# First attention in an audio tower: one sequence on 32 rows, four sequences side by side

## The chip, the cores and the metric

The kernel runs on one NeuronCore of a Trainium2 chip. The metric is the device time of one execution in microseconds (us), the median of several runs. A core has TensorE (matrix products, in the profile PE, its weight loads PEld), VectorE (DVE), ScalarE (ACT), GpSimd (POOL) and SyncE (SP), which run on their own and wait for one another by semaphores.

## The reference

64 sequences of 23 tokens go through a token layer, an attention with decaying gates, a routed feed-forward layer, a second attention and a quantized feed-forward layer. The change is in the first attention, which has 8 key heads of 128 dimensions, each with two query heads:

```python
logG = jnp.cumsum(log_g, axis=1)                       # per sequence and head
qk = jnp.einsum('bthd,bshd->bhts', q, k) * scale
a = qk ** 2
gate = logG[:, :, :, None] - logG[:, :, None, :]
a = jnp.where(causal, a * jnp.exp(gate), 0.0)
norm = jnp.sum(a, axis=-1) + 1e-06
y = jnp.einsum('bhts,bshd->bthd', a, v)
y = y / jnp.transpose(norm, (0, 2, 1))[..., None]
return y.reshape(B, T, H * R * D) @ Wc + bc            # q, k, v are hidden_states @ Wq, Wk, Wv
```

## The kernel before

The 1472 tokens (T) are four chunks (CH) of 368 columns (CW), and a chunk is 16 sequences of 23 (SL). The loop runs over the 8 heads, and its body is written out for the four chunks, on each engine in its own order. g counts chunks over all heads.

Products with weights are exact to about fp32: each operand is a high and a low fp16 part, and `split3` makes three matmuls (lines 915 to 917). `head_project(g, c, j)` projects one of q0, q1, k, v (j = 0 to 3) of a chunk: 12 matmuls of 368 columns, into bank j % 2. `out_proj(g, c)` multiplies a finished chunk's result with Wc: four blocks of 6 matmuls, into banks 6 and 7 by turns. VectorE adds each block to the accumulator (`accumulate`, line 1553). `out_proj` waits at line 973 before each block until VectorE has added the block two before it, which used the same bank.

Four sequences (92 rows, AT) are handled as one block: scores for the 92x92 pairs, of which a mask leaves the causal ones within a sequence. In a chunk TensorE does the projections that are left (j from 2 or 1), scores (line 1000, k stationary, fp32), turns v (line 1006), the previous chunk's `out_proj`, the weighted sums of v (line 1021; the stationary operand is the weight matrix, and v has a 129th column of ones, so that the sum of weights comes with it), one projection of the next chunk, and then turns the results (line 1037). ScalarE moves q, k, v out of PSUM (`head_moved`, line 661), makes E = exp(gate) (674) and the square (677), moves the turned v (680) and the turned results as yT_hi (698). VectorE makes the gates (1570, 1574), the weights a = sq x E (1579), divides the results by their sums (1593 to 1595) and makes yT_lo (1601).

Other work stands in the same order: ScalarE and VectorE split weights for the next head (`unit_a_hi`, `unit_a_lo` to wa; `unit_b_hi`, `unit_b_lo` to wb) and of an expert in every second chunk (line 666, and `expert_lo` in three pieces, line 1387), and ScalarE sums absolute values (686). In the fourth chunk TensorE waits for wa_lo before it projects for the next head. The gates reach VectorE through memory: SP writes lgt to lgd and reads it back as gr, spread over the rows (lines 406, 408 and 419). A semaphore target counts from a start value: b_acc and b_ev start at 2, b_wc at 1; free(n) is n + 1 and ready(n) is n + 3.

## Time and profile before

| | us |
|---|---|
| median of three runs | 1438.3 |
| these runs | 1438.11 to 1441.32 |
| the profiled execution | 1435.07 |
| its span (first to last instruction) | 1433.3 |
| TensorE busy in the span | 1279.8 |
| VectorE busy | 915.9 |
| ScalarE busy | 639.1 |
| GpSimd busy | 231.4 |

The profile is of one execution. Its timeline gives each instruction's start, its duration, and in brackets how long the engine had been idle and who released it. Matmuls overlap, so a stream of them is read by the distance of starts, not by durations. A product of fp32 operands shows two records.

### The profile page before, as it was taken

What the parts mean: (1) busy time and instruction counts of PE and PEld (TensorE: products, weight loads), DVE (VectorE), ACT (ScalarE), POOL (GpSimd) and SP (SyncE); (2) the same over time, 40 slices, a digit from 0 to 9 for tenths busy, and PEclk for the clock granted to TensorE, in tenths of its full rate; (3) what the DMA queues carried; (4) which work ended last, traced back from release to release, by engine and by line L of the source; (5) the groups of instructions that cost most, each with busy time, mean ns of one, the idle gap of its engine ahead of it and who ended that gap; (6) DMA issues with size and microseconds to landing.
All of it is one profiled execution on the core that took longest, in us unless ns stands there. A gap on an engine that the chain in (4) does not pass through costs nothing.

```text
span 1433.3 us, 28634 instructions
## 1 busy us (share of the span) xinstructions
PE 1279.8 (89%) x9689; PEld 789.5 (55%) x9690; DVE 915.9 (64%) x1920; ACT 639.1 (45%) x1086; POOL 231.4 (16%) x280
## 2 busy tenths in 40 slices
PE   6999999999999999996789999999986787859997
PEld 2447667677676767664435444544533565424443
DVE  5993665656656665668864555445348676778886
ACT  3444444554444445542325444444532433246664
POOL 2220000000000000000013333333347610110000
PEclk9997999999999999995799999999997787889999
DMA  5211452433435352422325867876336620000000
GB/s 191 73 66 62 161 199 104 182 135 143 182 141 199 123 191 103 176 89 83 141 75 200 280 220 246 318 256 208 109 121 137 100 36 2 1 0 16 22 22 26
DMA packets 42699, 184.21 MB, mean 129 GB/s; under 512 B 8688, under 2 KB 9200, under 8 KB 34832
## 3 DMA queue, kind: packets, MB, share of 16 engines
q0 software_dynamic: 19744, 95.41, 20.1%
q1 hardware_dynamic: 19440, 75.41, 14.8%
q10 hardware_dynamic: 3456, 12.58, 2.5%
q8 instruction: 39, 0.64, 0.2%
q14 instruction: 20, 0.16, 0.0%
HBM read 135.65 MB, written 47.73 MB: 128 GB/s over the span
## 4 chain that ended last, share of the span: by engine, by line
PE 58%; DVE 19%; issue 11%; DMA 4%; POOL 3%; ACT 2%; DVEq 1%; SPq 0%; ACTq 0%; POOLq 0%
PE ps L915 14%; PE ps L917 14%; PE ps L916 14%; PE ps L1021 3%; PE ps L1000 3%; DMA wide<-wsp 2%; DVE ff L2022 2%; DVE amf L2029 1%; PE ps L1105 1%; PE ps L1037 1%; POOL h L519 1%; PE ps L1358 1%; DVE bst L1460 1%; PE ps L1340 1%; DVE wa_lo L1387 1%
## 5 line engine op out<-in xcount | busy, mean ns | idle before, releaser
L915 PE MATMUL ps<-nT_hi,wa_hi 128*128 128x368 f16 x576 | 189.5, 329 | 11.1 <-DVE wa_lo L1387 8.1
L916 PE MATMUL ps<-nT_lo,wa_hi 128*128 128x368 f16 x576 | 189.1, 328 | 0.0
L917 PE MATMUL ps<-nT_hi,wa_lo 128*128 128x368 f16 x576 | 188.7, 328 | 0.0
L661 ACT ACTIVATE qk<-ps 128x368 f32<-128x368 f32 x128 | 60.4, 477 | 130.6 <-PE ps L917 130.5
L1751 DVE SCALAR_TENSOR_TENSOR nrm<-ps,xg,nrm 128x256 f32<-128x256 f32 x61 | 29.5, 484 | 123.8 <-ACT nrm L729 108.4
L915 PE MATMUL ps<-wide,xT 128*128 x244 | 92.7, 380 | 15.5 <-issue 12.3
L503 POOL DMA_INDIRECT xg<-xrow,idx x61 | 61.3, 1005 | 265.2 <-PE ps L1105 123.5
L1579 DVE TENSOR_TENSOR a<-sq,E 92x368 f32<-92x368 f32 x64 | 32.7, 538 | 107.1 <-ACT sq L677 107.1
L1553 DVE SCALAR_TENSOR_TENSOR wide<-ps,wide 128x368 f32<-128x368 f32 x128 | 69.3, 542 | 49.0 <-PE ps L917 49.0
L916 PE MATMUL ps<-wide,xT 128*128 x244 | 92.5, 379 | 0.0
L917 PE MATMUL ps<-wide,xT 128*128 x244 | 92.5, 379 | 0.0
L1340 PE MATMUL ps<-qw,qT 128*128 128x512 bf16 x384 | 88.7, 385 | 2.6 <-DVE ff L2022 2.6
L698 ACT ACTIVATE yT_hi<-ps 128x368 f16<-128x368 f32 x64 | 28.7, 476 | 134.7 <-PE ps L1037 134.7
L915 PE MATMUL ps<-yT_hi,wb_hi 128*128 128x368 f16 x256 | 82.5, 322 | 1.2 <-DVE yT_lo L1601 1.2
L915 PEld LDWEIGHTS ps<-nT_hi,wa_hi 128*128 128x128 f16 x576 | 57.8, 100 | 45.3 <-issue 17.4
L916 PE MATMUL ps<-yT_lo,wb_hi 128*128 128x368 f16 x256 | 82.4, 322 | 0.0
L917 PE MATMUL ps<-yT_hi,wb_lo 128*128 128x368 f16 x256 | 82.4, 322 | 0.0
L498 POOL DMA_DIRECT2D wsp<-we_sp x16 | 8.6, 540 | 433.8 <-DVE we_sp L1387 433.8
L917 PEld LDWEIGHTS ps<-nT_hi,wa_lo 128*128 128x128 f16 x576 | 57.7, 100 | 36.5 <-issue 4.6
L916 PEld LDWEIGHTS ps<-nT_lo,wa_hi 128*128 128x128 f16 x576 | 57.8, 100 | 31.8 <-issue 3.8
L731 ACT ACTIVATE hh<-nrm 128x256 f16<-128x256 f32 x73 | 30.4, 416 | 92.3 <-DVE nrm L1751 92.3
L482 POOL TENSOR_TENSOR rt_out<-rt_in,neg_half 128x1 f32<-128x1 f32 (+3 forms) x54 | 33.2, 616 | 231.6 <-DVE rt_in L1399 231.6
(312 smaller groups left out, 3098.3 us busy)
## 6 DMA issues: line engine op xcount, KB each, us to landing
we_st<-in_we POOLq DMA_DIRECT2D x16, 1536.0 KB, 6.7
wsp<-we_sp POOLq DMA_DIRECT2D x16, 1536.0 KB, 5.3
wide<-wsp SPq DMA_DIRECT2D x16, 1536.0 KB, 7.6
yslot<-yt POOLq DMA_DIRECT2D x61, 256.0 KB, 4.3
wq_st<-in_ffq SPq DMA_DIRECT2D x24, 512.0 KB, 4.2
wq_st<-in_ffq ACTq DMA_DIRECT2D x24, 512.0 KB, 3.6
wide<-in_wa SPq DMA_DIRECT2D x10, 1024.0 KB, 6.1
xt<-in_x SPq DMA_DIRECT2D x12, 512.0 KB, 3.4
```

Source lines behind the costliest of these rows:

```text
L482: nc.gpsimd.tensor_tensor(dst, src, neg_half[:, 0:src.shape[1]], ALU.pow).then_inc(done, 1)
L503: pool.indirect_dma_start(Q["xg"][:, g % 4, :].bitcast(U32), None, xrow, bass.IndirectOffsetOnAxis(ap=idx[:, g:g + 1], axis=0)).then_inc(x ...
L661: nc.scalar.activation(B["qk"][:, j, :], ps[:, j % 2, 0:CW], ACT.Copy, scale=(AS if j == 3 else 1.0) / WS).then_inc(b_ev, 1)
L731: nc.scalar.activation(Q["hh"][:, p, 0, :], ht, ACT.Copy).then_inc(m_hi, 1)
L915: nc.tensor.matmul(dst, lhs[0], rhs[0], start=start, stop=False)
L916: nc.tensor.matmul(dst, lhs[0], rhs[1], start=False, stop=False)
L917: return nc.tensor.matmul(dst, lhs[1], rhs[0], start=False, stop=stop)
L1000: ins = nc.tensor.matmul(ps[0:AT, 2 + j, a * REP * AT:(a + 1) * REP * AT], B["qk"][:, 2, tok], B["qk"][:, 0:2, tok], start=True, stop=True)
L1021: ins = nc.tensor.matmul(ps[0:AT, 4 + 2 * j + a, r * (DH + 1):(r + 1) * (DH + 1)], B["a"][0:AT, j, a, r, :], B["v1"][0:AT, 2 * j + a, :], ...
L1340: ins = nc.tensor.matmul(ps[:, 2 * (f % 2) + q, :], Gm["qT"][:, b, ds(k * P, P)], qw[:, q, b * FF + f * 512:b * FF + (f + 1) * 512], start ...
L1553: V.scalar_tensor_tensor(acc, ps[:, 6 + blk % 2, 0:CW], 1.0 / (WS * AS), acc, ALU.mult, ALU.add).then_inc(b_acc, 1)
L1579: V.tensor_tensor(B["a"][0:AT, j], B["sq"][0:AT, j], B["E"][0:AT, 2 * j:2 * j + 2].unsqueeze(2).broadcast_to([AT, 2, REP, AT]), ALU.mult). ...
```

## The change

Each sequence gets 32 rows of its own, with rows 23 to 31 zero, and four sequences (q = 0 to 3) lie side by side on the 128 rows. a = 0 to 3 counts such groups in a chunk, so a chunk's sequence is n = 4a + q.

- k and v are moved into tiles with 32 columns a sequence (kp, vp), whose last 9 stay zero.
- Scores are one product for each sequence: 32 rows of keys by 2 x 23 queries, 16 in a chunk. All lie in one half bank of 128 rows and 184 columns. So gates, exp, square and a are computed for 128x92 or 128x184 numbers, where it was 92x368 and twice 92x368.
- A product with a block matrix of ones (blk) gives each column's sum of weights on all rows of its sequence. Row 23 carries the 1e-6 (eps_row). VectorE takes the reciprocal of these 128x184 sums out of PSUM and multiplies the weights with it.
- The weighted sums have v stationary (32 rows by 128 dimensions) and the weights moving (46 columns), 16 products in a chunk. The results have dimensions as rows, so nothing is turned back; yT_hi and yT_lo are made from them, with columns put back in token order.
- `out_proj` of the previous chunk is cut in halves (blocks 0 and 1, then 2 and 3), with the sum of weights between them. VectorE's accumulations are cut into block 0, block 1, and blocks 2 and 3. Line 973's wait stays as it is.
- ScalarE makes the next head's wa_hi before the absolute values, not after.
- The gates are written to memory by q, and read back by four transfers a head onto 23 rows each. VectorE sets kp, vp, gr and blk before the loop.

```diff
-        lgd = nc.dram_tensor("lgd", (HEADS, T), F32, kind="Internal").ap()
+        lgd = nc.dram_tensor("lgd", (4, HEADS * 16, SL), F32, kind="Internal").ap()
...
+        def windows(y, x):
+            return y[:].rearrange("p r t -> p (r t)").rearrange("p (n q s) -> p q n s", q=4, s=SL)[:, 2 * x:2 * x + 2]
+        def weighted(x):
+            return ps[:, 2 + 2 * x:4 + 2 * x, 0:REP * AT].rearrange("p q (n s) -> p q n s", s=SL)
...
-            sp.dma_start(lgd.rearrange("h (a p) -> (h a) p", p=AT), B["lgt"][:, :]).then_inc(init_out, 16)
+            sp.dma_start(lgd.rearrange("q n s -> n q s"), B["lgt"][:].rearrange("p (q s) -> p q s", q=4)).then_inc(init_out, 16)
             sp.wait_ge(init_out, 32)
-            sp.dma_start(B["gr"][0:AT], lgd[0:1, :].broadcast_to([AT, T])).then_inc(gr_in, 16)
-            sp.wait_ge(gr_in, 16)
+            def gates_spread(head):
+                for q in range(4):
+                    sp.dma_start(B["gr"][32 * q:32 * q + SL].rearrange("p a s -> p (a s)"),
+                                 lgd[q].rearrange("(h a) s -> h (a s)", h=HEADS)[head, :].broadcast_to([SL, AT * 4])).then_inc(gr_in, 16)
+            gates_spread(slice(0, 1))
+            sp.wait_ge(gr_in, 64)
...
+                gates_spread(ds(i + 1, 1))
...
-                nc.scalar.activation(B["qk"][:, j, :], ps[:, j % 2, 0:CW], ACT.Copy,
-                                     scale=(AS if j == 3 else 1.0) / WS).then_inc(b_ev, 1)
+                if j < REP:
+                    nc.scalar.activation(B["q"][:, j, :], ps[:, j % 2, 0:CW], ACT.Copy, scale=1.0 / WS).then_inc(b_ev, 1)
+                else:
+                    nc.scalar.activation(B["kp" if j == 2 else "vp"][:, :, 0:SL], ps[:, j % 2, 0:CW].rearrange("p (w s) -> p w s", s=SL),
+                                         ACT.Copy, scale=(AS if j == 3 else 1.0) / WS).then_inc(b_ev, 1)
...
-                    nc.scalar.activation(B["E"][0:AT], B["gt"][0:AT], ACT.Exp).then_inc(b_E, 1)
-                    for j in range(2):
-                        act.wait_ge(b_sc, 3 * g + j + 1)
-                        nc.scalar.activation(B["sq"][0:AT, j].rearrange("p a r t -> p (a r t)"), ps[0:AT, 2 + j, 0:2 * REP * AT],
-                                             ACT.Square, scale=float(DH) ** -0.5).then_inc(b_sq, 1)
-                    act.wait_ge(b_sc, 3 * g + 3)
-                    nc.scalar.activation(B["v1"][0:AT, :, 0:DH],
-                                         ps[0:AT, 1, :].rearrange("p (a b) -> p a b", a=4), ACT.Copy).then_inc(b_ev, 1)
+                    nc.scalar.activation(B["E"][:], B["gt"][:].rearrange("p a s -> p (a s)"), ACT.Exp).then_inc(b_E, 1)
+                    act.wait_ge(b_sc, 2 * g + 1)
+                    nc.scalar.activation(B["sq"][:].rearrange("p r x -> p (r x)"), ps[:, 2, REP * AT:2 * REP * AT],
+                                         ACT.Square, scale=float(DH) ** -0.5).then_inc(b_sq, 1)
+                    act.wait_ge(b_sc, 2 * g + 2)
+                    nc.scalar.activation(B["v1"][:].rearrange("p a d -> p (a d)"), ps[:, 1, :], ACT.Copy).then_inc(b_ev, 1)
+                    if c == CH - 1:
+                        unit_a_hi(i + 1, b_pj, 4 * CH * (i + 1))
...
-                    if c == CH - 1:
-                        unit_a_hi(i + 1, b_pj, 4 * CH * (i + 1))
...
-                        act.wait_ge(b_yt, 2 * g + j + 1)
-                        nc.scalar.activation(oh[:, :, j * 2 * AT:(j + 1) * 2 * AT],
-                                             ps[:, 2 + j, 0:CW].rearrange("p (r t) -> p r t", r=REP), ACT.Copy).then_inc(b_hi, 1)
+                    act.wait_ge(b_av, g + 1)
+                    for x in range(2):
+                        nc.scalar.activation(windows(B["yT_hi"], x), weighted(x), ACT.Copy).then_inc(b_hi, 1)
...
-            def out_proj(g, c):
+            def out_proj(g, c, blks=range(4)):
                 pe.wait_ge(b_lo, 2 * g + 4)
-                for blk in range(4):
+                for blk in blks:
...
-                        pe.wait_ge(b_lo, free(2 * g + j))
-                        for a in range(2):
-                            tok = slice((2 * j + a) * AT, (2 * j + a + 1) * AT)
-                            ins = nc.tensor.matmul(ps[0:AT, 2 + j, a * REP * AT:(a + 1) * REP * AT],
-                                                   B["qk"][:, 2, tok], B["qk"][:, 0:2, tok], start=True, stop=True)
-                        ins.then_inc(b_sc, 1)
+                    pe.wait_ge(b_lo, free(2 * g + 1))
+                    for a in range(4):
+                        for q in range(4):
+                            n = 4 * a + q
+                            out = ps[32 * q:32 * q + 32, 2, REP * AT:2 * REP * AT].rearrange("p (r a s) -> p r a s", r=REP, a=4)
+                            ins = nc.tensor.matmul(out[:, :, a, :], B["kp"][:, n, :], B["q"][:, :, n * SL:(n + 1) * SL],
+                                                   start=True, stop=True)
+                    ins.then_inc(b_sc, 1)
                     pe.wait_ge(b_ev, ready(5 * g + 3))
                     for a in range(4):
-                        ins = nc.tensor.transpose(ps[0:AT, 1, a * P:(a + 1) * P], B["qk"][:, 3, a * AT:(a + 1) * AT], ident[:])
+                        ins = nc.tensor.transpose(ps[:, 1, a * P:(a + 1) * P],
+                                                  B["vp"][:, 4 * a:4 * a + 4, :].rearrange("p w s -> p (w s)"), ident[:])
                     ins.then_inc(b_sc, 1)
                     if c == 0:
                         head_project(g + 1, 1, 0)
                     else:
                         if c == 1:
                             pe.wait_ge(wb_lo, i + 1)
-                        out_proj(g - 1, c - 1)
-                    pe.wait_ge(b_ev, ready(5 * g + 4))
-                    for j in range(2):
-                        pe.wait_ge(b_a, 2 * g + j + 1)
-                        if j == 1:
-                            pe.wait_ge(b_acc, 4 * g + 2)
-                        for a in range(2):
-                            for r in range(REP):
-                                ins = nc.tensor.matmul(ps[0:AT, 4 + 2 * j + a, r * (DH + 1):(r + 1) * (DH + 1)],
-                                                       B["a"][0:AT, j, a, r, :], B["v1"][0:AT, 2 * j + a, :],
-                                                       start=True, stop=True)
-                        ins.then_inc(b_av, 1)
+                        out_proj(g - 1, c - 1, (0, 1))
+                    pe.wait_ge(b_a, 2 * g + 1)
+                    nc.tensor.matmul(ps[:, 3, REP * AT:2 * REP * AT], B["blk"][:], B["a"][:].rearrange("p r x -> p (r x)"),
+                                     start=True, stop=True).then_inc(b_sm, 1)
                     if c == 0:
                         head_project(g + 1, 1, 1)
-                    elif c < CH - 1:
+                    else:
+                        out_proj(g - 1, c - 1, (2, 3))
+                    pe.wait_ge(b_ev, ready(5 * g + 4))
+                    pe.wait_ge(b_a, 2 * g + 2)
+                    for a in range(4):
+                        for q in range(4):
+                            w = slice(32 * q, 32 * q + 32)
+                            ins = nc.tensor.matmul(ps[:, 2 + q, 0:REP * AT].rearrange("p (r a s) -> p r a s", r=REP, a=4)[:, :, a, :],
+                                                   B["v1"][w, a, :], B["a"][w, :, a * SL:(a + 1) * SL], start=True, stop=True)
+                    ins.then_inc(b_av, 1)
+                    if 0 < c < CH - 1:
                         head_project(g + 1, c + 1, 0)
-                    elif not last:
+                    elif c == CH - 1 and not last:
                         pe.wait_ge(wa_lo, i + 2)
                         head_project(g + 1, 0, 0)
-                    for j in range(2):
-                        pe.wait_ge(b_yn, 2 * g + j + 1)
-                        for r in range(REP):
-                            for a in range(2):
-                                ins = nc.tensor.transpose(ps[:, 2 + j, (2 * r + a) * AT:(2 * r + a + 1) * AT],
-                                                          B["yn"][0:AT, j, a, r, :], ident[0:AT, 0:AT])
-                        ins.then_inc(b_yt, 1)
...
+            order(V.memset(B["kp"][:], 0.0))
+            order(V.memset(B["vp"][:], 0.0))
+            order(V.memset(B["gr"][:], 0.0))
+            order(V.memset(B["blk"][:], 0.0))
+            for q in range(4):
+                ins = V.memset(B["blk"][32 * q:32 * q + 32, 32 * q:32 * q + 32], 1.0)
+            order(ins)
...
-                    order(V.tensor_tensor(B["gt"][0:AT], B["gr"][0:AT, c * CW:(c + 1) * CW].rearrange("p (a t) -> p a t", a=4),
-                                          B["LGh"][0:AT, 4 * c:4 * c + 4].unsqueeze(2).broadcast_to([AT, 4, AT]), ALU.subtract))
+                    order(V.tensor_tensor(B["gt"][:], B["gr"][:, 4 * c:4 * c + 4, :],
+                                          B["LGh"][:, 4 * c:4 * c + 4].unsqueeze(2).broadcast_to([P, 4, SL]), ALU.subtract))
                     if c == CH - 1:
                         dve.sem_inc(b_gr, 1)
-                    V.tensor_tensor(B["gt"][0:AT], B["gt"][0:AT], mask[0:AT].unsqueeze(1).broadcast_to([AT, 4, AT]),
+                    V.tensor_tensor(B["gt"][:], B["gt"][:], mask[:].unsqueeze(1).broadcast_to([P, 4, SL]),
                                     ALU.add).then_inc(b_g, 1)
                     dve.wait_ge(b_E, g + 1)
-                    for j in range(2):
-                        dve.wait_ge(b_sq, 2 * g + j + 1)
-                        V.tensor_tensor(B["a"][0:AT, j], B["sq"][0:AT, j],
-                                        B["E"][0:AT, 2 * j:2 * j + 2].unsqueeze(2).broadcast_to([AT, 2, REP, AT]),
-                                        ALU.mult).then_inc(b_a, 1)
+                    dve.wait_ge(b_sq, g + 1)
+                    V.scalar_tensor_tensor(B["a"][:], B["sq"][:], eps_row[:, 0:1], B["E"][:].unsqueeze(1).broadcast_to([P, REP, AT]),
+                                           ALU.add, ALU.mult).then_inc(b_a, 1)
                     if c:
-                        accumulate(g - 1, c - 1)
+                        accumulate(g - 1, c - 1, (0,))
+                    dve.wait_ge(b_sm, g + 1)
+                    dve.sem_inc(passed, 1)
+                    order(V.reciprocal(B["rs"][:].rearrange("p r x -> p (r x)"), ps[:, 3, REP * AT:2 * REP * AT]))
+                    V.tensor_tensor(B["a"][:], B["a"][:], B["rs"][:], ALU.mult).then_inc(b_a, 1)
+                    if c:
+                        accumulate(g - 1, c - 1, (1,))
                     else:
                         unit_b_lo(i)
                     if c == CH - 1:
                         unit_a_lo(i + 1)
+                    if c:
+                        accumulate(g - 1, c - 1, (2, 3))
                     if c % 2:
                         expert_lo(2 * i + c // 2, 0)
-                    for j in range(2):
-                        dve.wait_ge(b_av, 2 * g + j + 1)
-                        y = ps[0:AT, 4 + 2 * j:6 + 2 * j, 0:REP * (DH + 1)].rearrange("p a (r d) -> p a r d", r=REP)
-                        order(V.tensor_scalar(B["rn"][0:AT, j], y[:, :, :, DH], 1e-6, None, ALU.add))
-                        order(V.reciprocal(B["rn"][0:AT, j], B["rn"][0:AT, j]))
-                        V.tensor_tensor(B["yn"][0:AT, j], y[:, :, :, 0:DH],
-                                        B["rn"][0:AT, j].unsqueeze(3).broadcast_to([AT, 2, REP, DH]), ALU.mult).then_inc(b_yn, 1)
-                    if c % 2:
                         expert_lo(2 * i + c // 2, 1)
-                    for j in range(2):
-                        dve.wait_ge(b_hi, 2 * g + j + 1)
-                        V.tensor_tensor(B["yT_lo"][:, :, j * 2 * AT:(j + 1) * 2 * AT],
-                                        ps[:, 2 + j, 0:CW].rearrange("p (r t) -> p r t", r=REP),
-                                        B["yT_hi"][:, :, j * 2 * AT:(j + 1) * 2 * AT], ALU.subtract).then_inc(b_lo, 1)
+                    for x in range(2):
+                        dve.wait_ge(b_hi, 2 * g + x + 1)
+                        V.tensor_tensor(windows(B["yT_lo"], x), weighted(x), windows(B["yT_hi"], x), ALU.subtract).then_inc(b_lo, 1)
```

## Rows read from the trace of the kernel before

**Rows 1.** The page: busy time with share of the span, by engine.
```profile
PE 1279.8 (89%) x9689; PEld 789.5 (55%) x9690; DVE 915.9 (64%) x1920; ACT 639.1 (45%) x1086; POOL 231.4 (16%) x280
```
**Rows 2.** Stretch: us; PE, PEld, DVE, ACT, POOL busy; PE clock, DMA share, GB/s.
```profile
200.00:300.00 100.00, 98.38 (x686) 71.30 (x685) 60.44 (x117) 47.11 (x82) 3.77 (x7) 1.00 0.39 149
```
**Rows 3.** Timeline of TensorE, a head's third chunk: start us, us taken, engine, line, operation.
```profile
362.60 1.41 PE L1000 MATMUL ps<-qk 128*92 128x184 f32 x8
363.85 0.60 PE L1006 MATMUL ps<-ident,qk 128*92 128x128 f32 x4
364.28 0.32 PE L915 MATMUL ps<-yT_hi,wb_hi 128*128 128x368 f16 x1
...
368.02 1.93 PE L1021 MATMUL ps<-v,a 92*92 92x129 f32 x16
369.79 0.32 PE L915 MATMUL ps<-nT_hi,wa_hi 128*128 128x368 f16 x1
...
377.91 1.41 PE L1000 MATMUL ps<-qk 128*92 128x184 f32 x8
```
**Rows 4.** Same view: a fourth chunk and the next head's first two; brackets: idle before.
```profile
314.29 1.41 PE L1000 MATMUL ps<-qk 128*92 128x184 f32 x8
...
322.80 0.33 PE L915 MATMUL ps<-nT_hi,wa_hi 128*128 128x368 f16 x1 [1.15 <-DVE wa_lo L1387]
...
335.57 1.41 PE L1000 MATMUL ps<-qk 128*92 128x184 f32 x8
...
347.14 1.41 PE L1000 MATMUL ps<-qk 128*92 128x184 f32 x8
```
**Rows 5.** Timeline at the stage's start: VectorE, then TensorE.
```profile
143.61 0.54 DVE L1570 TENSOR_TENSOR gt<-gr,LGh 92x368 f32<-92x368 f32 x1 [8.36 <-DMA gr<-lgd]
...
146.52 2.23 PE L1021 MATMUL ps<-v,a 92*92 92x129 f32 x16 [3.01 <-ACT v L680]
```
**Rows 6.** Timeline of TensorE, the last head's fourth chunk.
```profile
632.42 1.41 PE L1000 MATMUL ps<-qk 128*92 128x184 f32 x8
...
646.00 0.49 PE L915 MATMUL ps<-yT_hi,wb_hi 128*128 128x368 f16 x1 [1.16 <-DVE yT_lo L1601]
```
**Rows 7.** Timeline of TensorE, short products of the second attention.
```profile
1103.94 0.23 PE L1224 MATMUL ps<-wb_lo,nT_hi 128*32 128x128 f16 x4
1104.00 0.23 PE L1224 MATMUL ps<-wb_hi,nT_lo 128*32 128x128 f16 x4
...
1147.12 3.77 PE L1246 MATMUL ps<-kr,qp 32*128 32x23 f32 x128 [0.65 <-DVE qp L1884]
...
1156.09 0.32 PE L917 MATMUL ps<-nT_hi,wa_lo 128*128 128x368 f16 x1
1156.34 1.66 PE L1273 MATMUL ps<-wide,V 32*32 32x92 f32 x128
1157.93 0.33 PE L915 MATMUL ps<-nT_hi,wa_hi 128*128 128x368 f16 x1
```
**Rows 8.** Timeline of ScalarE in the chunk of rows 3.
```profile
362.80 0.48 ACT L661 ACTIVATE qk<-ps 128x368 f32<-128x368 f32 x1 [1.39 <-PE ps L917]
```
**Rows 9.** Groups by shape: line, engine, operation, shapes, count | busy us, mean ns | idle.
```profile
L1664 DVE RECIPROCAL rt<-rt 128x192 f32<-128x192 f32 x1 | 1.4, 1353 | 0.0
...
L1553 DVE SCALAR_TENSOR_TENSOR wide<-ps,wide 128x368 f32<-128x368 f32 x128 | 69.3, 542 | 49.0 <-PE ps L917 49.0
...
L1387 DVE SCALAR_TENSOR_TENSOR wa_lo<-wide,wa_hi 128x2048 f16<-128x2048 f32 x10 | 22.8, 2281 | 2.7 <-ACT wa_hi L594 2.7
...
L1387 DVE SCALAR_TENSOR_TENSOR we_sp<-we_st,we_sp 128x1024 f16<-128x1024 f32 x48 | 58.3, 1215 | 0.3
```
**Rows 10.** Stretches of TensorE alone: us, busy, granted clock, DMA share, GB/s.
```profile
148.00:152.00 4.00, 4.00 (x19) 0.57 0.94 379
320.00:324.00 4.00, 2.85 (x23) 1.00 0.96 334
1112.00:1116.00 4.00, 2.67 (x52) 0.50 0.87 130
```

60 lines of the change are left out of this document (31 added, 29 removed).

## The prediction, made from the kernel before alone

> **What bounds the kernel now.** I read the page's busy shares first [rows 1]: TensorE 89% of the span, VectorE 64%. Then the table of busy time by stretches: in the stage that changes (the first attention, about 140 to 650 us) TensorE is busy 98 of 100 us at full clock [rows 2]. So a chunk there lasts as long as TensorE's instruction stream, plus what TensorE waits. The timeline of one chunk (third of its head) shows the stream [rows 3]: scores start at 362.60, the next chunk's at 377.91, 15.31 us. An output projection is 24 matmuls, 3.74 us (364.28 to 368.02), 0.156 each; a block of 6 is 0.93, a projection of 12 is 1.87. 72 such matmuls are 11.2 us; the remaining 4.1 us are what the change touches: scores 1.25, v turned 0.43, weights times values 1.77 (368.02 to 369.79), results turned back 0.64, by difference.
>
> The last chunk of a head is different [rows 4]: TensorE stands idle 1.15 us for the next head's low weights (wa_lo), and a little later for yn. From the fourth chunk's scores (314.29) to the next head's first (335.57) it is 21.28 us; that head's first chunk takes 11.57 and the second 15.46 (to 362.60). A head is 63.6 us. Start and end stand apart: TensorE idles 3.01 us before the first weighted sums, because the gates' rows land late and VectorE waits 8.36 us for them [rows 5]; the last head needs 646.00 - 632.42 = 13.58 us from its last scores to its last output projection [rows 6].
>
> **The change, part by part.** I count t from the start of a chunk's scores.
>
> *Scores.* 4 products of 184 columns become 16 of 46, in 32-column strips, each two passes (fp32 shows two records a product: x8 for four [rows 3]): 32 pairs of weight load and matmul. The trace has two relatives [rows 7]. In the second attention 128 pairs of 32x32 fp32 take 1157.93 - 1156.34 = 1.59 us, 12 ns a pair. Four side by side over all 128 rows, as here, exist in fp16: groups of four pairs start every 0.06 us, 14 to 15 ns a pair. Low bound 32 x 0.012 = 0.4 us. Upper: a pass streams 38 ns (184 columns take 0.156, a quarter) and its load is at most 27 ns (128 columns are hidden in the 0.108 us that a turning matmul takes, a quarter of that); were nothing overlapped, 32 x 0.065 = 2.1 us. I take 0.45, nearest to the four-abreast row, and 0.1 for entering this shape (1156.09 to 1156.34 is 0.25 where 0.156 is usual). But turning v needs v moved out of PSUM: ScalarE starts that at t = 0.20 and takes 0.48 [rows 8], so t = 0.73 with the signal. Scores shorter than 0.73 gain no more. So 1.25 becomes 0.73.
>
> The Trainium skill (TensorE: Matmul & The Clock Gate, Part 3, packing small matmuls) says that a weight load overlaps running matmuls only when its row group differs, and all scores here use all rows. That speaks for the 2.1 us end; the fp16 strips of this trace, with all rows too, speak against it.
>
> *v turned* stays 0.43 (fp32, 128 columns either way).
>
> *Sum of weights.* New: one product of 184 columns, two passes, 0.31 us, in the stream. It starts after half the cover: t = 0.73 + 0.43 + 1.87 = 3.03. Its result is visible at 3.03 + 0.16 + 0.32 + 0.04 = 3.55. The weights it needs are done by t = 1.6 (E and the square, each short, then one VectorE step), so no wait before it.
>
> *Dividing.* VectorE now takes the reciprocal of 128x184 numbers. Reciprocals are not priced like other operations: 128x192 took 1353 ns [rows 9], where a simple step on 368 elements takes 542 (so 192 some 350). I take 1.30. Then the product, 0.26 until the next instruction can start (542 - 184 x 1.04 = 0.35, less 0.09 of overlap that consecutive instructions show). On VectorE: reciprocal 3.55 to 4.85, product 4.89 to 5.24.
>
> *The new wait.* The output projection of the previous chunk is cut in halves, and VectorE's accumulations too: block 0, then the two dividing steps, then block 1. Block 3 on TensorE uses block 1's bank and must wait for its accumulation (line 973). TensorE comes to block 3 at t = 3.34 + 0.93 = 4.27; VectorE accumulates block 1 from 5.15 to 5.69 (0.54). So block 3 starts at 5.74: a stall of 1.47 us, with the weighted sums and the next projections queued behind it. This falls on the second, third and fourth chunk of each head. In the first chunk a projection stands in the place, to 5.21, and the weighted sums wait for the product till 5.28.
>
> *Weighted sums.* 8 products of 129 columns over 92 rows become 16 of 46 over 32 rows, four abreast: 32 pairs with a 128-column load. The relative is the second attention's scores (32 rows, 128-column load, 23 columns): 128 in 3.77 us, 29 ns each with the tail, at full clock [rows 7]. With 23 columns more in one row strip of four, 19/4 = 5 ns more at most. 32 x 0.028 to 0.033, 0.9 to 1.05, and 0.1 to 0.2 for changing shape in and out: 1.15, against 1.77. If loads did not overlap, 32 x (0.038 + 0.027) = 2.1.
>
> *Results.* Nothing is turned: 0.64 gone, and the yn steps on VectorE with it. The moves to yT_hi and yT_lo keep size.
>
> *Sums.* First chunk: 0.73 + 0.43 + 1.87 + 0.31 + 1.94 + 1.15 + 3.73 = 10.16 (before 11.57): -1.41. Second and third: 5.74 + 0.93 + 1.15 + 4 x 1.87 = 15.29 (before 15.46 and 15.31): -0.17 and -0.02. There the whole gain of the stream (about 1.5) is given back by the stall.
>
> Fourth: weighted sums end at 7.82. VectorE, after block 1, makes wa_lo (2.28 [rows 9]) 5.60 to 7.88; ScalarE's part of it, moved ahead of the absolute values, is done by t = 4. TensorE goes on at 7.93, two projections to 11.66. VectorE meanwhile accumulates blocks 2 and 3 (to 8.7), splits two pieces of the expert (1215 ns each, 1.13 apart, to 10.95) and then yT_lo, to 11.92. The output projection starts at 11.97 (stall 0.3), and 4 x 1.87 later, 19.43, come the next head's scores (before 21.28): -1.85. That gain is mostly the old two waits at this place.
>
> Heads: -(1.41 + 0.17 + 0.02) x 8 = -12.8; fourth chunks -1.85 x 7 = -13.0; the last one 13.58 to 11.97, -1.6. Start: the gates' rows were one transfer to 92 rows of 5.9 KB, and become four to 23 rows of 1.5 KB, a quarter of the bytes; against it stand three more issues, and a write in 512 pieces of 92 bytes. VectorE waited 8.36 us for write and read together [rows 5]; if the read shrinks with its bytes, they land over 3 us earlier. I count all of the 3.01 us of idle, -3.0; the ends are 0 (the pieces eat it) and -3.0. The memsets on VectorE there, about 1500 columns at 1.04 ns, up to 1.6 us, lie in its wait for ScalarE's logarithm; uncovered they would cost that once. Gates for later heads are asked for at the head's fourth chunk, as before, a whole output projection and two projections ahead. SP issues three transfers more a head, after the weight loads, and nothing is queued behind them before the next head. Together -30.4.
>
> *Clock.* The second attention's bursts of short products are followed by half clock: 0.50 in 1112:1116, after a burst at 1109. But a wait of 1.15 us beside weighted sums (320:324) stayed at 1.00. After the start's 3 us wait it fell to 0.57 over 4 us, 1.7 us of work lost [rows 10]. The new chunks put a 1.47 us stall, one block, and a burst of short products next to each other, 24 times. I count 5 falls of 1.7 us, +8.5; ends 0 and 24 falls, +41.
>
> Sum -30.4 + 8.5 = -21.9. The profiled execution took 1435.07 us; 1413.2 after. The median of the runs shown is 3.2 higher (1438.3), so I forecast **1416 us**.
>
> **The rivals.**
> 1. *Weight loads of the strips do not overlap.* What the skill's rule says for scores. Scores 2.1 + 0.1 instead of 0.73: +1.45 x 32 = +46, giving 1462, slower than before. It decides from 0.85 us more a chunk (27/32), that is scores over 1.6 us. For it: no fp32 strip over all rows is in the trace. Against: rows 7. Chance 0.07.
> 2. *The clock falls in nearly each of the 24 stalls.* +41 - 8.5: 1449, slower. For it: the burst in rows 10. Chance 0.10; a middle count, or the weighted sums unoverlapped ((2.1 + 0.1 - 1.15) x 32 = +33, 1449 too, or half of it), within 0.3% or slightly above: 0.12.
> 3. *The reciprocal costs like any other vector step (0.35 us).* Then block 1 is ready at 4.74 and the stall is 0.5, no clock falls: -0.95 x 24 - 8.5: 1385. Against: the 1353 ns row. Chance 0.05.
> 4. *Loads of scores serial, but beside the stream* (27 ns each, 0.96 us): +0.23 x 32 = +7, 1423; inside the forecast.
> 5. *The stage is bound elsewhere and nothing moves.* Against: TensorE's 98%. It is in the 0.12 above.
>
> **How the numbers follow.** Forecast 0.66 (1400 to 1432: no falls 1408, cheapest sums 4 less, ten falls and serial loads 1432). Cases 1 and 2 slower 0.17, middle 0.12, case 3 0.05. Range 1396 to 1442. About 0.3% (4.3 us) can be told from no change. Faster: 0.66 + 0.05 + a part of the middle, 0.73. Same 0.11. Slower 0.16.
>
> **What would show it.** In the profile after: scores x32 in 0.4 to 0.6 us with v's turning at t = 0.73 (if 2 us, rival 1); the reciprocal near 1300 ns; TensorE idle before line 915's block 3 of the output projection, released by VectorE's accumulation, about 1.5 us, 24 times (if absent, my order of waits is wrong); weighted sums x32 in about 1 us; the idle before the first weighted sums gone; granted clock by stretches in 150:640, whether 1.00 or with halves. The prediction would be wrong most by the size of the stall or by the clock. The sign would be wrong if two of the small costs (strips, clock, reciprocal from PSUM) add up.

## The result, and the profile after

The medians are 1438.2 us before and 1426.55 after; the ratio is 0.9919 with a 95% interval of 0.9895 to 0.9944. So the kernel is 11.7 us faster, where 22 were forecast: the sign was right, and the gain about half. The profiled execution of after, which all lines here come from, took 1428.67 us and was the slowest of its four (1423.78 the fastest), so between the two profiled executions the difference is only 1435.07 - 1428.67 = 6.4 us. The terms below are summed against that.

The page of after, busy time by engine, against [rows 1]:

```profile
span 1426.5 us, 30564 instructions
PE 1241.8 (87%) x10777; PEld 717.1 (50%) x10778; DVE 866.0 (61%) x1767; ACT 614.0 (43%) x1054; POOL 230.9 (16%) x280
```

TensorE works 38 us less, VectorE 50 us less, and the time shrinks by 6 to 12. The gain went into waiting. The timeline of TensorE over a head's second chunk, with the next chunk's first row, answers to [rows 3]:

```profile
280.67 0.54 PE L1022 MATMUL ps<-q,kp 128*32 128x46 f32 x32
281.31 0.66 PE L1028 MATMUL ps<-ident,vp 128*128 128x128 f32 x4
...
283.67 0.47 PE L1038 MATMUL ps<-a,blk 128*128 128x184 f32 x2
...
286.49 0.33 PE L935 MATMUL ps<-yT_hi,wb_hi 128*128 128x368 f16 x1 [1.41 <-DVE wide L1579]
...
287.53 1.10 PE L1049 MATMUL ps<-a,v 32*128 32x46 f32 x32
...
296.15 0.54 PE L1022 MATMUL ps<-q,kp 128*32 128x46 f32 x32
```

The stream is what was forecast: scores 0.54 us instead of 1.41, the sum of weights 3.00 us after the scores' start, the weighted sums in 1.10. At 286.49, in the middle of the output projection, stands the new wait of 1.41 us, put down to VectorE's accumulation (line 1579). From scores to scores it is 15.48 us; before it was 15.46 for a second chunk and 15.31 for a third.

VectorE in the chunk that follows shows what the wait is made of:

```profile
298.42 0.54 DVE L1579 SCALAR_TENSOR_TENSOR wide<-ps,wide 128x368 f32<-128x368 f32 x1 [0.77 <-PE ps L937]
299.78 1.31 DVE L1611 RECIPROCAL rs<-ps 128x184 f32<-128x184 f32 x1 [0.82 <-PE ps L1038]
301.12 0.35 DVE L1612 TENSOR_TENSOR a<-a,rs 128x184 f32<-128x184 f32 x1
301.39 0.98 DVE L1579 SCALAR_TENSOR_TENSOR wide<-ps,wide 128x368 f32<-128x368 f32 x2
```

Block 0 is accumulated at 298.42. Then VectorE is idle for 0.82 us, until the sum of weights is there, divides for 1.6 us, and only then (301.39) takes block 1, whose result has been waiting in PSUM. TensorE needs that bank for block 3.

The second thing that is new in the stage is the granted clock. The table by stretches, TensorE alone, against [rows 2] (us, busy and instructions, granted clock, DMA share, GB/s):

```profile
200.00:600.00 400.00, 369.24 (x3642) 0.97 0.41 155
162.00:166.00 4.00, 4.00 (x19) 0.59 0.01 4
```

Nine times in the stage's 24 stalls the clock falls to its lower level (1.2 GHz); 162:166 holds most of the first. Six of these falls lie in second and third chunks, which then take 17.12 us instead of 15.48 (1.64 us lost), three in fourth chunks, which take 20.9 instead of 19.78 (1.13 lost). Together that is 13.2 us.

### The profile page after: what moved, and what is told of

Read it like the earlier page. It is cut to its first block, busy times and chain, and to the rows that moved or that the text cites. A ratio compares the mean times of both kernels' runs of the same rounds, so it can differ in the third digit from the quotient of the medians.

```text
span 1426.5 us, 30564 instructions
## 1 busy us (share of the span) xinstructions
PE 1241.8 (87%) x10777; PEld 717.1 (50%) x10778; DVE 866.0 (61%) x1767; ACT 614.0 (43%) x1054; POOL 230.9 (16%) x280
## 4 chain that ended last, share of the span: by engine, by line
PE 52%; DVE 25%; issue 12%; ACT 4%; POOL 3%; DVEq 2%; DMA 1%; another core or an unknown queue 0%; SPq 0%; ACTq 0%; POOLq 0%
PE ps L935 14%; PE ps L937 13%; PE ps L936 13%; DVE rs L1611 2%; PE ps L1049 2%; POOL h L539 2%; DVE ff L2045 2%; DVE amf L2052 2%; PE ps L1028 1%; DVE nrm L1774 1%; PE ps L1376 1%; PE ps L1358 1%; DVE bst L1478 1%; PE ps L1123 1%; ACT vp L682 1%
## 5 line engine op out<-in xcount | busy, mean ns | idle before, releaser
L935 PE MATMUL ps<-nT_hi,wa_hi 128*128 128x368 f16 x576 | 195.6, 340 | 3.9 <-DVE nT_lo L1442 3.0
L936 PE MATMUL ps<-nT_lo,wa_hi 128*128 128x368 f16 x576 | 194.4, 338 | 0.0
L937 PE MATMUL ps<-nT_hi,wa_lo 128*128 128x368 f16 x576 | 193.5, 336 | 0.0
L1605 DVE SCALAR_TENSOR_TENSOR a<-sq,eps_row,E 128x184 f32<-128x184 f32 x32 | 13.1, 409 | 141.8 <-ACT sq L699 141.8
L740 ACT ACTIVATE xT<-ps 128x1024 f16<-128x1024 f16 x61 | 62.3, 1023 | 16.9 <-PE ps L1123 9.1
```

The costliest lines, as they stand in the source:

```text
L740: nc.scalar.activation(Q["xT"][:, p].rearrange("p a b -> p (a b)"), ps[:, p, :].bitcast(F16), ACT.Copy).then_inc(m_xe, 1)
L935: nc.tensor.matmul(dst, lhs[0], rhs[0], start=start, stop=False)
L936: nc.tensor.matmul(dst, lhs[0], rhs[1], start=False, stop=False)
L937: return nc.tensor.matmul(dst, lhs[1], rhs[0], start=False, stop=stop)
```

## Experiments

Medians of runs taken at different times are compared by their ratio to the kernel before, which ran beside each. After stands at 0.9919.

### Is the stall the order of VectorE's steps?

My theory: block 1's accumulation stands behind the division only because it was written there, and VectorE is idle before the reciprocal anyway (0.82 us above). Rival: something else holds the next projections, and the stall goes elsewhere.

```diff
                     if c:
-                        accumulate(g - 1, c - 1, (0,))
+                        accumulate(g - 1, c - 1, (0, 1))
                     dve.wait_ge(b_sm, g + 1)
...
-                    if c:
-                        accumulate(g - 1, c - 1, (1,))
-                    else:
+                    if not c:
                         unit_b_lo(i)
```

> The changed kernel, with one VectorE step moved: the accumulation of output block 1 stands before the wait for the sums of weights, not behind the two dividing steps. Theory (the 1.41 us stall of TensorE before block 3 is that accumulation, and the stall also brings the clock down): block 3 does not wait; the weighted sums wait 0.3 us for the divided weights instead (reciprocal from t = 3.75, product done 5.44, TensorE there at 5.19). Second and third chunks 15.48 to about 14.1 us; fourth chunks only 19.8 to 19.3, since wa_lo and then yT_lo on VectorE come last there. That is -22 to -26 us, and no falls of the granted clock to half in the stage (9 before, about 1.6 us each), together 1380 to 1392. Rival A (the clock falls because of the short products, not of the stall): falls stay, about 1400. Rival B (the stall has another cause, for instance TensorE's shape changes): no change, 1427.

Measured: 1392.67 us, ratio 0.9668 (0.9638 to 0.9699), 2.5% below after. Its stretch 200:600 (all engines: PE, PEld, DVE, ACT, POOL busy, clock, DMA share, GB/s) and TensorE's waits in 200:620 (us in total, times, longest):

```profile
200.00:600.00 400.00, 382.46 (x3920) 248.28 (x3917) 218.90 (x368) 188.41 (x326) 14.55 (x27) 1.00 0.42 157
```

```profile
PE ps L935 <- DVE wa_lo L1405: 6.6, 6, 1.1
```

The waits for line 1579 inside the output projection (28.3 us in 20, below) are gone. What comes instead: second and third chunks take 14.11 us (the next kernel shows that they could take 13.90; the weighted sums wait about 0.2 for the product, not the 0.3 expected), the fourth 19.36, where the old wait for wa_lo is back at 1.1 us; it had been hidden behind the stall. The clock in 200:600 is 1.00 with one fall (at 480) where after has six. From the chunks: 16 x (15.48 - 14.11) + 7 x (19.78 - 19.36) = 24.9 us, and nine falls of 13.2 us together against one of 1.3 (this kernel's 20.69 instead of 19.36), 11.9: in all 36.8 us. The spans differ by 36.7. One fall was left where none was expected.

### Is it the reciprocal's price?

In this kernel a copy stands in place of the reciprocal, so the division is left out: the weights are multiplied with their sum. The dependences stay.

```diff
-  order(V.reciprocal(B["rs"][:].rearrange("p r x -> p (r x)"), ps[:, 3, REP * AT:2 * REP * AT]))
+  order(V.tensor_copy(B["rs"][:].rearrange("p r x -> p (r x)"), ps[:, 3, REP * AT:2 * REP * AT]))
```

> The changed kernel with the reciprocal of the sums replaced by a plain copy of them (the weights are multiplied by their sums and not divided, which is left out of the computation). It measures the reciprocal's price on the path. Theory: the copy of 128x184 takes about 0.34 us against 1.31, so everything behind it on VectorE comes 0.97 us earlier: stall before block 3 0.44 instead of 1.41, 24 times, -23 us, and few or no falls of the clock (another -15): 1388 to 1404. Rival: the stall hangs on something other than VectorE's chain, then no change.

Measured: 1396.53, ratio 0.9689 (0.9656 to 0.9723). TensorE's wait in 200:620, after first and then this kernel:

```profile
PE ps L935 <- DVE wide L1579: 28.3, 20, 1.4
```

```profile
PE ps L935 <- DVE wide L1579: 9.6, 21, 0.5
```

and the steps themselves (groups by shape: count | busy us, mean ns | idle before), of after and of this kernel:

```profile
L1611 DVE RECIPROCAL rs<-ps 128x184 f32<-128x184 f32 x27 | 35.3, 1307 | 31.2 <-PE ps L1038 31.2
```

```profile
L1611 DVE COPY rs<-ps 128x184 f32<-128x184 f32 x28 | 9.8, 349 | 32.0 <-PE ps L1038 32.0
```

958 ns less in the step, 0.95 us less in the wait: all of the reciprocal's extra lies on the path. None of the 24 stalls is followed by a fall of the clock (the one fall in the stage comes after the wait at its start, 0.50 in 148:150), so a stall of 0.46 us beside the same short products leaves it up. Rival 3 of the prediction said that a cheap reciprocal would give just this chunk; it fell by 1307 ns.

### Does the stall bring the clock down, or do the short products?

In after, nine idle matmuls (1.57 us, into a bank that nobody reads then) fill the stall. Nothing else changes; the wait stays, TensorE only works through it.

```diff
-                        out_proj(g - 1, c - 1, (2, 3))
+                        out_proj(g - 1, c - 1, (2,))
+                        for _ in range(9):
+                            nc.tensor.matmul(ps[:, 0, 0:CW], wb[0][:, 0, 0:P], nT[0][:, 0, 0:CW], start=True, stop=True)
+                        out_proj(g - 1, c - 1, (3,))
```

> The changed kernel with 9 idle matmuls (128x368 fp16, 1.40 us, results unused, into a free bank) put on TensorE between output blocks 2 and 3 of the second to fourth chunks, just where it stalls for 1.41 us. They cost no time by themselves. It tells apart what brings the clock down. Theory (the stall does): no falls to half clock in the stage, about -15 us, 1411 to 1415. Rival (the bursts of short products do): falls stay about 9, time 1425 to 1430.

Measured: 1418.02, ratio 0.9848 (0.9817 to 0.9879): adding work made the kernel 0.7% faster than after.

```profile
200.00:600.00 400.00, 394.51 (x3917) 252.14 (x3916) 209.28 (x353) 178.96 (x311) 14.51 (x27) 1.00 0.41 156
```

The clock is 1.00 instead of 0.97 and the stage has no falls. A third chunk takes what it took in after, 15.49 us (291.65 to 307.14), so the filling costs nothing and nearly the whole difference is the clock: 13.8 us between the spans, where nine falls are 13.2. But of after the slowest of four executions was profiled, and of this kernel the fastest; by the medians the gain is 8.5 us, by the ratios 10, and 1418.02 lies outside the 1411 to 1415 that I expected. So the short products alone don't bring the clock down; with a 1.41 us stall among them it falls in some places. A second profile with the same 24 stalls (the kernel with two queues, below) shows eight falls, again at places of its own.

The same from the other side: a kernel without the stall in which the weighted sums are issued twice (the second pass writes the same values again). Its base is the next step, the kernel with block 1 first and with the weighted sums moved behind the projection of head g + 1 in second and third chunks:

```diff
                         out_proj(g - 1, c - 1, (2, 3))
+                    if 0 < c < CH - 1:
+                        head_project(g + 1, c + 1, 0)
                     pe.wait_ge(b_ev, ready(5 * g + 4))
...
-                    if 0 < c < CH - 1:
-                        head_project(g + 1, c + 1, 0)
-                    elif c == CH - 1 and not last:
+                    if c == CH - 1 and not last:
```

> e1_block1_first and in the second and third chunks the weighted sums moved behind the next chunk's first projection (1.87 us), so that the divided weights are long ready. Theory: e1 less its remaining wait of 0.3 us in 16 chunks, 4 to 5 us below e1; second and third chunks about 13.9 us; fourth as in e1. Rival (e1's remaining wait is not there, or the results come too late for the next scores): no better than e1, or worse.

Measured: 1391.18, ratio 0.965 (0.9618 to 0.9682). The wait went: second and third chunks take 13.90 us. That is 16 x 0.21 = 3.4 us, and the median is only 1.5 us below that of the kernel with block 1 first: the profile has three falls (190, 364 and 480 us) where that one had one, and two more falls are 2.7 us. The kernel was run again:

> e5_sums_later once more, for the number of times the granted clock falls to half in the stage. Its first profile showed 3, e1_block1_first's 1, e7's none, though none of them has the 1.41 us stall. Theory (the falls need a stall beside short products, and e5's fourth chunk has two of 1.1 and 0.3 us around its weighted sums): again 1 to 4, with the same time as before (1391). Rival (their number is chance without relation to the order): anything from 0 to 9.

Measured: 1387.21, ratio 0.9664 (0.9633 to 0.9694), three falls again, two of them at other places (247, 364, 538 us). Then the doubled sums:

```diff
-                    for a in range(4):
+                    for a in (0, 1, 2, 3, 0, 1, 2, 3):
```

> e5_sums_later with the weighted sums issued twice (32 more short fp32 pairs a chunk, 32 chunks, the same results), no stall added. It measures their price uncovered, and whether bursts of short products bring the clock down without a stall. Theory: 32 pairs at 0.033 us (1.10 us for a burst in the trace) are +1.0 us a chunk, +32 to +34 us, 1423 to 1426, with no more than the few falls that e5 had. Rival (short products alone bring the clock down): a dozen or more falls in the stage at 1.6 us, 1440 or above.

Measured: 1409.27, ratio 0.9786 (0.9761 to 0.9812), some 18 us above its base. I had expected 1423 to 1426, a miss by 14 us: I charged every chunk with the second pass at 1.0 us. It costs 0.9, in fourth chunks it hides in the wait for wa_lo (19.36 us in both kernels), which falls from 1.1 to 0.2, and the base's three falls, 1.3 us each, are not there.

```profile
250.78 2.00 PE L1051 MATMUL ps<-a,v 32*128 32x46 f32 x64
...
252.98 0.33 PE L935 MATMUL ps<-nT_hi,wa_hi 128*128 128x368 f16 x1 [0.20 <-DVE wa_lo L1405]
```

64 pairs take 2.00 us where 32 take 1.10: 0.90 / 32 = 0.028 us a pair, the price of the second attention's scores [rows 7]. And the clock in 200:600 is 1.00, without a fall, though the bursts are twice as long. What the runs show is nine and eight falls in the chunks with the 1.41 us stall, and none to three without it. The seven falls that two kernels without it show in three profiles (block 1 first, and twice the sums moved) all lie in fourth chunks, which there wait 1.1 us for wa_lo. But the kernel before waits 1.15 us at the same place and shows none there, and the kernel with wa_lo halved (below), whose fourth chunks wait 1.47 us between two output blocks, away from short products, shows none there either. So neither the length of a wait nor its place has been shown to decide a single fall; that stays open.

### Did ScalarE's moved step matter?

The change also makes wa_hi before the absolute values. Done alone in the kernel before:

```diff
                                          ps[0:AT, 1, :].rearrange("p (a b) -> p a b", a=4), ACT.Copy).then_inc(b_ev, 1)
+                    if c == CH - 1:
+                        unit_a_hi(i + 1, b_pj, 4 * CH * (i + 1))
...
-                    if c == CH - 1:
-                        unit_a_hi(i + 1, b_pj, 4 * CH * (i + 1))
```

> The kernel before with one part of the change alone: ScalarE makes the next head's wa_hi before the absolute values, 1.2 us earlier. Theory: nothing, since VectorE comes to wa_lo only after its four accumulations (in the trace of before wa_hi ended at 383.1 and wa_lo began at 383.99): the same time as before within 0.3%. Rival: the wait for wa_lo (1.15 us a head) falls by up to all of it, -8 us, ratio 0.994.

Measured: 1438.36, ratio 0.9994 (0.9974 to 1.0014). Nothing, and the wait that it might have shortened is what the kernel before has too, 6.9 us in 6:

```profile
PE ps L915 <- DVE wa_lo L1387: 6.9, 6, 1.2
```

So wa_lo waits for VectorE's own queue of work, not for ScalarE's part. Nor did the absent steps on yn shorten it: with block 1 first the wait is back at 1.1 us. What hid it in after is that TensorE arrives later, by the stall. That the step is worth nothing in the changed kernel too was not run.

### Why did a quarter of the bytes not arrive sooner?

For the stage's start I had forecast 3.0 us of gain, and the wait there grew instead. Memory traffic while the gates are read: before (137:144), then after (138:145).

```profile
GB/s 0 0 0 0 135 135 135 0 135 135 101 34 135 135 101 67 67 135 135 101 34 135 135 135 34 101 135 135 135 34 101 135 135 34 0 0 0 0 0 0
DMA packets 96, 0.54 MB, mean 77 GB/s; under 512 B 4, under 2 KB 4, under 8 KB 96
```

```profile
GB/s 0 0 0 17 25 25 25 25 17 8 0 0 17 25 25 25 25 25 25 25 25 25 25 25 25 25 25 25 25 25 25 25 25 25 25 25 17 17 0 0
DMA packets 96, 0.14 MB, mean 19 GB/s; under 512 B 4, under 2 KB 96, under 8 KB 96
```

92 rows in both. Before, a row of 5888 bytes took 0.225 us and about four moved at a time; after, a row of 1472 bytes takes about 0.06 us and they move singly, at 25 GB/s. The time is nearly the same. My theory: the rows of one queue go singly here, so two queues halve it. Rival: the memory row that all 23 copies read from is the limit. In this kernel SP issues two of the four reads, and GpSimd's queue the two others, for the first head only. The edit, shortened:

```diff
-            gates_spread(slice(0, 1))
-            sp.wait_ge(gr_in, 64)
+            gates_spread(slice(0, 1), range(2))
+            sp.wait_ge(gr_in, 32)
...
+                if e == 0:
+                    pool.wait_ge(init_out, 32)
+                    for q in (2, 3):
+                        pool.dma_start(B["gr"][32 * q:32 * q + SL].rearrange("p a s -> p (a s)"),
+                                       lgd[q].rearrange("(h a) s -> h (a s)", h=HEADS)[0:1, :].broadcast_to([SL, AT * 4])).then_inc(gr_two, 16)
...
+            dve.wait_ge(gr_two, 32)
```

> The changed kernel, where two of the first head's four transfers of gates come from GpSimd's queue and two from SP's. The changed kernel's 92 rows of 1472 bytes came one after another, 0.06 us each, and VectorE had its gates at 145.0 us, 9.7 us after it was ready, against 143.6 before. Theory (the rows of one queue go one at a time): the two halves run beside each other and the gates are there 2 to 2.7 us earlier, near 142.5, and the wait before the first sums of weights (3.45 us) falls by as much. Rival (one place in memory or one transfer engine serves all the rows): no earlier than 145. Seen in the trace, not in the total (0.2%).

Measured: 1425.36, a single run. The memory traffic (137:144), SP's issue, and VectorE's first steps with the gates:

```profile
GB/s 0 0 0 0 0 0 0 0 0 8 0 25 25 25 143 85 109 101 8 0 9 25 25 25 25 17 25 25 25 25 17 0 0 0 0 0 0 0 94 281
```

```profile
137.69 0.60 SPq L425 DMA_DIRECT2D gr<-lgd  x2
...
143.14 0.18 DVE L1596 COPY LGh<-LG 128x16 f32 x1 [7.59 <-DMA gr<-lgd]
143.56 0.26 DVE L1602 TENSOR_TENSOR gt<-gr,LGh 128x92 f32<-128x92 f32 x1 [0.25 <-DVE LGh L1596]
```

From issue to gates 5.45 us, where after takes 7.80 (137.24 to 145.04, below), and the wait before the first sums of weights is 1.39 us instead of 3.45, as expected. SP's 46 rows still go singly, GpSimd's took about 1 us together (the slices of 85 to 143 GB/s), though 23 of them again read one memory row. So the memory row is not the limit. That it is the queue as such is not shown: SP's queue moved the 92 long rows of before four at a time, and those came in one transfer of 92 rows, not in four of 23. Neither the number of rows in a transfer nor their length was changed alone. The time of the whole kernel can't tell 1.5 us in a single run; the lines can.

### What is the whole shape worth once its waits are mended?

First the fourth chunk. Of wa_lo only the columns for q are needed at once. The half for k and v goes behind yT_lo, and one piece of the expert with it; base is the kernel with the sums moved. The edit, shortened:

```diff
+            def unit_a_lo_half(n, x):
+                dve.wait_ge(wa_hi, n + 1)
+                cols = slice(256 * x, 256 * x + 256)
...
                     if c == CH - 1:
-                        unit_a_lo(i + 1)
+                        unit_a_lo_half(i + 1, 0)
...
+                    if c == CH - 1:
+                        unit_a_lo_half(i + 1, 1)
                     if c % 2:
+                        expert_lo(2 * i + c // 2, 1)
```

> e5_sums_later with VectorE's wa_lo for the next head cut in two: the half for q (1.2 us) where it stood, the half for k and v behind yT_lo; and the expert's second piece behind yT_lo too. Theory (in e5 the fourth chunk is VectorE's chain: TensorE waits 1.1 us for wa_lo and 0.3 for yT_lo): both waits go, 1.4 us in seven chunks, -10 us, and with them the three falls of the clock that e5 still had (-5): 1376 to 1382. Rival (the clock's falls in e5 have another cause, or VectorE's later pieces come too late for the next head): gain under 5 us.

Measured: 1387.89, ratio 0.964 (0.9615 to 0.9664), a miss by 6 us. Both waits are gone, and one of their size stands behind them, so that fourth chunks take 19.59 us where the base has 19.36; the 3 us gained are the base's falls of the clock. The last output projection's block 2 waits until block 0 is accumulated, and VectorE is still at the expert's pieces. Waits in 200:580, and one of them in the timeline:

```profile
PE ps L935 <- DVE wide L1586: 8.8, 6, 1.5
```

```profile
197.28 0.33 PE L935 MATMUL ps<-yT_hi,wb_hi 128*128 128x368 f16 x1 [1.47 <-DVE wide L1586]
```

So the accumulation of blocks 0 and 1 goes before the last piece, and the two queues for the first gates are added:

```diff
                         expert_lo(2 * i + c // 2, 1)
+                        if c == CH - 1:
+                            accumulate(g, c, (0, 1))
                         expert_lo(2 * i + c // 2, 2)
...
-                accumulate(g, c)
+                accumulate(g, c, (2, 3))
```

> e7_wa_lo_halves with two mends. In e7 the waits for wa_lo and yT_lo went, as expected, but a new one came: TensorE waited 1.47 us in seven fourth chunks for the accumulation of the last output projection's block 0, queued on VectorE behind the half of wa_lo and two expert pieces. Here blocks 0 and 1 are accumulated ahead of the last expert piece. Theory: these 1.47 us go, -10 us. And the first head's gates come over two queues as in e6, -2 us. Together 1375 to 1379. Rival (yet another item on VectorE comes last): 1383 or more.

Measured: 1371.64 us (1370.01 to 1374.16), ratio 0.9554 (0.9532 to 0.9576). This beats both kernels, by 4.5% and 3.7%. It is 3.4 us under the 1375 to 1379 that I expected; the kernel before, run beside it, was 2.6 us faster than in the first comparison. Its stretch 200:560, and a whole head of it by first scores:

```profile
200.00:560.00 360.00, 355.64 (x3660) 1.00 0.45 167
```

```profile
254.26 0.54 PE L1029 MATMUL ps<-q,kp 128*32 128x46 f32 x32
...
264.60 0.54 PE L1029 MATMUL ps<-q,kp 128*32 128x46 f32 x32
...
278.50 0.54 PE L1029 MATMUL ps<-q,kp 128*32 128x46 f32 x32
...
292.40 0.54 PE L1029 MATMUL ps<-q,kp 128*32 128x46 f32 x32
...
310.46 0.54 PE L1029 MATMUL ps<-q,kp 128*32 128x46 f32 x32
```

TensorE is busy 98.8% of the stretch at full clock. Chunks take 10.34, 13.90, 13.90 and 18.06: a head is 56.2 us, where before has 63.6 [rows 4] and after 61.1.

## Why the prediction was right or wrong

Direction and mechanism held, and the measured time lies in the stated range; the sum was off in the size of three terms (the chunks, the clock, the start). By the prediction's own steps:

*Scores and v.* v's turning at t = 0.73 was forecast and comes at 0.64; the scores' 32 pairs took 0.54 us with the tail (280.67), and v's turning 0.49 instead of 0.43. Rival 1 (loads of strips not overlapped, 2.1 us) fell. The Trainium skill (TensorE: Matmul & The Clock Gate, Part 3) ties that overlap to different row groups; here all strips use all rows and a pair costs at most 0.54 / 32 = 0.017 us, so the measurement decides against it for column strips. Rival 4 fell with it.

*Sum of weights, division, stall.* At t = 3.00 (forecast 3.03); reciprocal 1.307 us (1.30), product 0.35 (0.35), block 3 at t = 5.82 (5.74); stall 1.41 (1.47), released by the accumulation, in the second, third and fourth chunk. The first two experiments show each link: with the order changed the stall is gone, with a cheap step in the reciprocal's place it shrinks by the difference. This part is shown, not argued.

*Weighted sums.* 1.15 forecast; 1.10 with the tail.

*Chunks.* First 10.16 forecast, 10.34 measured (270.33 to 280.67); second 15.29 and 15.48; third 15.29 and 15.49; fourth 19.43 and 19.78 (250.55 to 270.33). Each is 0.18 to 0.35 too low. Of that, 0.08 stands before block 3, and about 0.1 is TensorE's change of shape into the scores (250.30 to 250.55 below is 0.25 where 0.156 is usual). I had priced it, but inside the scores' estimate, which lay below 0.73 and so stood in no sum. In the fourth both forecast waits are there, by difference some 0.2 us for wa_lo (0.11 forecast) and 0.3 for yT_lo (0.3), but each ends 0.19 later than forecast: TensorE goes on at t = 8.12 and its output projection starts at 12.16, for 7.93 and 11.97. Over the stage the four differences are 8 x (0.18 + 0.19 + 0.19) + 7 x 0.35 = 6.9 us, the largest of my misses, and the least visible of them.

```profile
250.30 0.32 PE L937 MATMUL ps<-nT_hi,wa_lo 128*128 128x368 f16 x1
250.55 0.54 PE L1022 MATMUL ps<-q,kp 128*32 128x46 f32 x32
...
256.38 0.33 PE L935 MATMUL ps<-yT_hi,wb_hi 128*128 128x368 f16 x1 [1.41 <-DVE wide L1579]
257.42 1.10 PE L1049 MATMUL ps<-a,v 32*128 32x46 f32 x32
...
270.33 0.54 PE L1022 MATMUL ps<-q,kp 128*32 128x46 f32 x32
```

*The last head.* 11.97 us from scores to output projection forecast, 12.09 measured (625.94 to 638.03), against 13.58 before [rows 6].

*The start.* Forecast -3.0, measured about -0.9; this step failed. The wait did not vanish but grew, from 3.01 [rows 5] to 3.45 us:

```profile
145.04 0.25 DVE L1596 TENSOR_TENSOR gt<-gr,LGh 128x92 f32<-128x92 f32 x1 [9.67 <-DMA gr<-lgd]
```

```profile
146.69 0.58 PE L1038 MATMUL ps<-a,blk 128*128 128x184 f32 x2 [3.45 <-DVE a L1605]
```

The sentence at fault is "if the read shrinks with its bytes". The gates come 1.43 us later (145.04 against 143.61), in three parts:

```profile
134.70 0.41 SPq L420 DMA_DIRECT2D lgd<-lgt  x1
...
137.24 1.27 SPq L425 DMA_DIRECT2D gr<-lgd  x4
```

The write is issued 0.25 us later (134.70, 134.45 before), behind the memsets, which were not quite covered. From write to read it is 2.54 us where before had 1.71 (134.45 to 136.16): 0.83 for the 512 pieces. And from the read's issue to the gates 7.80 against 7.45: 0.35, for a quarter of the bytes. The -0.9 has another source. The first chunk of all takes 14.07 us where it took 16.49; less the ordinary -1.23 of a first chunk that is -1.19, and first scores are 0.27 later (140.07, before 139.80). In that -1.19 is the work that before lost to the half clock after its wait, 1.7 us [rows 10], and against it stands the longer wait. That the clock stayed up there is luck, not the change: the kernel with the copy and the one with wa_lo halved start in the same way, but their clock fell (0.50 in 148:150), and their first chunks take 15.31 and 15.70 us. And the kernel before with ScalarE's step moved, otherwise the same at this place, kept its clock up and took 14.59 us for its first chunk, where before took 16.49. What I had as an end of that term ("the ends are 0") was nearer than the value I chose.

*The clock.* Forecast 5 falls of 1.7 us, +8.5; measured 9, six of 1.64 and three of 1.13, +13.2. The size of one was nearly right, the count was not, and nothing in the rows of before could fix it between 0 and 24. Rival 2 came true in 9 of its 24 places. That the stall and not the short products is what matters was shown by the third experiment and the doubled sums.

*The sum.* (-1.23 + 0.02 + 0.17) x 8 = -8.3; fourth chunks -1.50 x 7 = -10.5; last head -1.5; start -0.9; clock +13.2. Together -8.0, which is what the stage gained up to its last output projection (638.03 against 646.00). The profiled executions differ by 6.4: the other 1.6 us were lost behind that point or outside the spans, where the change touches nothing, and are not explained. Against the forecast's -21.9 the stage's miss of 13.9 is 6.9 from the chunks, 4.7 from the clock, 2.1 from the start and 0.1 from the last head. By the medians the whole miss is 10.5 us. How often the clock fell in the runs without a profile is not known; their mean granted clock over the whole kernel, 0.933 to 0.935, is that of the profiled one (0.934).

*What the prediction did not ask.* It worked out that the stall gives back the stream's gain in second and third chunks. It did not ask whether the stall's cause had to be there. VectorE's idle time of 0.82 us ahead of the reciprocal, which follows from its own numbers (block 0 done before 3.0, sum of weights visible at 3.55), had room for most of the accumulation that the stall waits for. That one line is worth 2.5%, three times what the whole change brought.

## What to carry to other kernels

When a slow step of VectorE is put between the halves of a projection, list which PSUM bank each block behind it reuses, and put every accumulation that frees a bank ahead of the slow step. Count a stall of TensorE beside short products twice, once for itself and once for the clock that it may cost (here a fall after 9 and 8 of 24), and expect that each wait that is removed uncovers the next one on the same engine, here three in a row (for block 1, wa_lo and block 0). A transfer spread in rows is not priced by its bytes alone: here the bytes fell to a quarter, the rows went singly instead of four at a time, and nothing was won.

## What the runs showed of the hardware that was not expected

- Rows of 1472 bytes read from one memory row onto 23 partitions each went singly through SP's queue, about 0.06 us each at 25 GB/s; rows of 5888 bytes, one transfer to 92 partitions, took 0.225 us each but some four at a time, at up to 135 GB/s. 46 of the short rows on GpSimd's queue took about 1 us. Why SP's queue takes the short rows singly (their length, 23 rows a transfer, the queue) stays open.
- Four 32-column strips over all 128 rows, fp32: 32 pairs of load and matmul in 0.54 us with the tail. With 32 rows and 128-column loads: 0.028 us a pair.
- A reciprocal of 128x184 from PSUM takes 1307 ns, a copy of the same 349 ns.
- 1.57 us of idle matmuls in a stall made the kernel 0.7% faster, by keeping TensorE at 2.4 GHz. 24 stalls of 1.41 us gave nine falls in one profile and eight in another, 24 of 0.46 us none. Two kernels without the stall still show one to three falls, all in fourth chunks, in places that differ from run to run; what decides them stays open.
